# Centring image 0 ahead of the bias tables, a fourth warming product, and the step table made inside pairs 3 to 6

## The chip, the cores and the metric

One core of a Trainium2 chip runs the kernel. The metric is the device time of one execution in microseconds (us), as the median of several runs. The engines are TensorE (PE in the rows, with its weight loads as PEld), VectorE (DVE), ScalarE (ACT), GpSimd (POOL) and SyncE (SP), which here issues transfers. Each engine works through its own queue in order, and they wait for each other by semaphores.

## The reference

The input x is 4 images of 64 channels and 32 x 32 positions, in float32. Two blocks with residual additions follow each other.

```python
# 1: a layer norm over channels, then local attention over 7x7 windows
x = x + conv(ln_c(x), wq, wk, wv, rel_x, rel_y)
#    q, k, v = 1x1 projections; logits = q . k over the window + bias_x + bias_y
#    (from q and the two tables of relative positions); softmax over 49; mix v
# 2: 1024 tokens an image, a layer norm over channels, then 33 steps of a routed network
t = tokens(x)
t = t + ffn(ln_t(t), ...)
def step(h, p):
    op = argmax(h[0, 0, :19])            # one of 19 operations, from the state itself
    y = attention(h, wq[op], wk[op], wv[op]) @ wo[op];  h = where(attn_mask[op], y, h)
    z = relu(h @ w1[op] + b1[op]) @ w2[op] + b2[op];    h = where(ffn_mask[op], z, h)
```

At most steps both masks of the chosen operation are off and the state stays as it is. So the kernel makes a step table: for each operation and each step, the next step at which one of the two masks is on, and which of them.

## The kernel before

The work is a written-out queue for each engine. Channels lie on partitions, and two images lie above each other, so that [128, 1024] holds a pair of images; "image 0" below is the first such pair (x0_loaded) and "image 1" the second (x1_loaded). Both together are four quarters of 512 columns, numbered 0 to 3.

**The head** makes the normalised images for the first attention. For quarter j, centre(j) is one product of 128 x 128 by 512 columns on TensorE (x minus its mean over channels, L332), square(k, j) on ScalarE squares it (L750) and copies it out (L752), variance(k, j) on TensorE sums (L341), root(k, j) on ScalarE takes the root (L756), inverse(k, j) on VectorE the reciprocal (L1012), spread(k, j) on TensorE spreads it over the channels (L350), and scale(k, j) on VectorE multiplies (L1023). Then come the query products (L380), the bias products (biases, L401 and L404) and the scores.

TensorE's queue begins with three warming products of 512 columns on zeros (L362). Behind them it waits for the three small loads behind t_loaded (w_qk, w_q, bias_tables), turns the key weights (L366), makes the bias tables (L368), waits for ScalarE's copy of the turned keys (wk_copied, L769), folds the key weights into the query weights (L372) and signals tab_ready. Only then come centre(0), centre(1), variance(0, 0), the wait for image 1, centre(2), variance(0, 1), spread(0, 0), the wait for the copied tables (tab_copied), spread(0, 1), centre(3) and so on. ScalarE's queue has the key copy, the four table copies (L772, L774), and then square(0, 0), square(0, 1), root(0, 0), square(0, 2), root(0, 1), four copies of masks (L786), square(0, 3).

VectorE's queue has make_table() ahead of inverse(0, 0): thirteen small instructions (L993 to L1006) on 19 partitions, each but the last waited for by the next through dve_step. The last signals table_ready; SyncE writes the table out (L257) and reads it back as one row (L259). Its readers are all at the first decision, behind pair 15.

**The pairs.** The first attention is 16 pairs of blocks, p = 0 to 15. In round p TensorE turns the probabilities of pair p (L466), turns the values of pair p + 1 (L455), makes the scores of pair p + 2 (L441, L445) and mixes pair p (L478). VectorE's queue in round p is normalise(p + 1) (L1062, L1065), copy_values(p + 1) (L1074), maxima(p + 2) (L1056), add_mixed(p) (L1082). ScalarE takes the exponentials (L813) and copies (L824), and GpSimd copies the values of a pair (L313).

**Behind the pairs** come the second norm and the steps of the routed network.

Of the kernel before, what the change touches and what calls it, by code (L numbers as in the profile page):

```python
# [28 lines left out]
P = 128  # L29
C = 64  # L30
# [11 lines left out]
TX, TY = 32 + KC - 1, 32 + KR - 1  # L42
NBLK = NPOS // (BR * BC)
NB, NOPS, HID = 33, 19, 256
# [12 lines left out]
def build(nc, x, w_qk, w_q, w_v, bias_tables, key_onehot, masks, ident, mean_mat, spread_mat, iotas,  # L57
          attn_mask, ffn_mask, attn_pack, ffn_w1, ffn_pack, out):
    with ExitStack() as ctx:
# [3 lines left out]
        def sem(name):  # L63
            return ctx.enter_context(nc.semaphore(name))

        ps = ctx.enter_context(nc.psum_tensor("ps", [P, 8, 512], F32))


        eye = sb("eye", [P, P])
# [7 lines left out]
        wqk = sb("wqk", [C, P])  # L77
        wqk_bd = sb("wqk_bd", [P, P])
        wq_nat = sb("wq_nat", [C, C])
        wk_nat = sb("wk_nat", [C, C])  # L80
        wv_bd = sb("wv_bd", [P, P])
        rel_tab = sb("rel_tab", [C, TX + TY])
# [31 lines left out]
        ahead = sb("ahead", [NOPS, 2, 2 * NB])  # L114
        ahead_i = sb("ahead_i", [NOPS, NB + 1], I32)
# [34 lines left out]
        S = {n: sem(n) for n in names}  # L150
# [178 lines left out]
        def _(pe):  # L329
            def centre(j):  # L330

                nc.tensor.matmul(ps[:, j, :], centre_w[:], x2f[:, j * 512:j * 512 + 512],  # L332
                                 start=True, stop=True).then_inc(S["centred"], 1)

            def variance(k, j):

                pe.wait_ge(S["squared"], 4 * k + j + 1)
                if j >= 2:
                    pe.wait_ge(S["h_ready" if k else "normed"], j - 1)
                for s in range(4):  # L340
                    mm = nc.tensor.matmul(ps[32 * s:32 * s + 32, 4 + 2 * (j % 2), 0:P], mean_w[:, P:P + 32],  # L341
                                          sq[:, j * 512 + P * s:j * 512 + P * s + P], start=True, stop=True)
                mm.then_inc(S["var_ready"], 1)
# [14 lines left out]
                                     start=True, stop=True)  # L358

            pe.wait_ge(S["idle_set"], 1)  # L360
            for i in range(3):
                nc.tensor.matmul(ps[:, 6, :], idle_in[:, 0:P], idle_in[:], start=True, stop=True)  # L362

            pe.wait_ge(S["t_loaded"], 48)
            pe.wait_ge(S["eye_loaded"], 16)
            nc.tensor.transpose(ps[0:C, 5, 0:C], wqk[:, C:P], eye[0:C, 0:C]).then_inc(S["wk_turned"], 1)  # L366
            for h in range(2):
                nc.tensor.matmul(ps[C * h:C * h + C, 7, 0:TX + TY], wq_nat[:], rel_tab[:],  # L368
                                 start=True, stop=True)
            pe.wait_ge(S["wk_copied"], 1)  # L370
            for h in range(2):
                mm = nc.tensor.matmul(ps[C * h:C * h + C, 7, P:P + C], wq_nat[:], wk_nat[:],  # L372
                                      start=True, stop=True)
            mm.then_inc(S["tab_ready"], 1)

            def queries(j):

# [33 lines left out]
            pe.wait_ge(S["x0_loaded"], 32)  # L411
            centre(0)
            centre(1)
            variance(0, 0)
            pe.wait_ge(S["x1_loaded"], 32)
            centre(2)
            variance(0, 1)
# [325 lines left out]
        def _(act):  # L743
            def load_table(func):

                nc.scalar.activation(spare[:, 0:1], eps_c[:, 0:1], func)

            def square(k, j):
                act.wait_ge(S["centred"], 4 * k + j + 1)
                nc.scalar.activation(sq[:, j * 512:j * 512 + 512], ps[:, j, :],  # L750
                                     ACT.Square).then_inc(S["squared"], 1)
                nc.scalar.copy(xc[:, j * 512:j * 512 + 512], ps[:, j, :]).then_inc(S["centre_copied"], 1)  # L752

            def root(k, j):
                act.wait_ge(S["var_ready"], 4 * k + j + 1)
                nc.scalar.activation(sq[:, j * 512:j * 512 + P], ps[:, 4 + 2 * (j % 2), 0:P], ACT.Sqrt,  # L756
                                     bias=eps_c[:, k:k + 1]).then_inc(S["std_ready"], 1)
# [6 lines left out]
            act.dma_start(x2[C:P, 1], x_parts[1][1]).then_inc(S["x1_loaded"], 16)  # L764
            act.wait_ge(S["eps_set"], 1)
            load_table(ACT.Sqrt)
            act.wait_ge(S["w_zeroed"], 1)
            act.wait_ge(S["wk_turned"], 1)
            nc.scalar.copy(wk_nat[:], ps[0:C, 5, 0:C]).then_inc(S["wk_copied"], 1)  # L769
            act.wait_ge(S["tab_ready"], 1)  # L770
            for h in range(2):
                nc.scalar.copy(tabs[C * h:C * h + C, h, :], ps[C * h:C * h + C, 7, 0:TX + TY]  # L772
                               ).then_inc(S["tab_copied"], 1)
                nc.scalar.copy(wqk_bd[C * h:C * h + C, C * h:C * h + C], ps[C * h:C * h + C, 7, P:P + C]  # L774
                               ).then_inc(S["tab_copied"], 1)
            square(0, 0)
            square(0, 1)
            root(0, 0)
            square(0, 2)
            root(0, 1)  # L780
            act.wait_ge(S["c_loaded"], 64)
# [189 lines left out]
        def _(dve):  # L971
# [7 lines left out]
            dve.wait_ge(S["eye_loaded"], 16)  # L979
            nc.vector.tensor_tensor(centre_w[:], eye[:], mean_w[:, 0:P], ALU.subtract).then_inc(S["centre_ready"], 1)  # L980

            def make_table():


                steps = [0]

                def step(ins):
                    steps[0] += 1
                    ins.then_inc(S["dve_step"], 1)
                    dve.wait_ge(S["dve_step"], steps[0])  # L990

                dve.wait_ge(S["m_loaded"], 48)
                step(nc.vector.memset(ahead[:], 4.0 * NB))  # L993
                step(nc.vector.tensor_copy(kinds[:], masks8[:]))
                step(nc.vector.scalar_tensor_tensor(kinds[:, 0, :], kinds[:, 1, :], 2.0, kinds[:, 0, :],
                                                    ALU.mult, ALU.add))
                step(nc.vector.tensor_scalar(kinds[:, 1, :], kinds[:, 0, :], 0.0, 4.0 * NB,
                                             ALU.is_equal, ALU.mult))
                step(nc.vector.tensor_tensor(kinds[:, 0, :], kinds[:, 0, :], iota[:], ALU.add))
                step(nc.vector.tensor_tensor(ahead[:, 0, 0:NB], kinds[:, 0, :], kinds[:, 1, :], ALU.max))  # L1000
                by, at = 1, 0
                while by < NB:
                    step(nc.vector.tensor_tensor(ahead[:, 1 - at, 0:NB], ahead[:, at, 0:NB],
                                                 ahead[:, at, by:by + NB], ALU.min))
                    by, at = 2 * by, 1 - at
                nc.vector.tensor_copy(ahead_i[:], ahead[:, at, 0:NB + 1]).then_inc(S["table_ready"], 1)  # L1006

            def inverse(k, j):

                rstd = sq[:, j * 512:j * 512 + P]  # L1010
                dve.wait_ge(S["std_ready"], 4 * k + j + 1)
                nc.vector.reciprocal(rstd, rstd).then_inc(S["inv_ready"], 1)  # L1012

            def scale(k, j, done="normed"):
                at, bank = j * 512, 4 + 2 * (j % 2)
                dve.wait_ge(S["centre_copied"], 4 * k + j + 1)
                dve.wait_ge(S["spread_ready"], 4 * k + j + 1)
                if k == 0:
                    r0 = 16 * (j % 2)
                    dst = h_in[:, j // 2, r0:r0 + 16, :].rearrange("p (b r) w -> p b r w", b=2)  # L1020
                else:
                    dst = h2[:, at:at + 512].rearrange("p (b r w) -> p b r w", b=2, w=WW)
                nc.vector.tensor_tensor(dst,  # L1023
                                        xc[:, at:at + 512].rearrange("p (b r w) -> p b r w", b=2, w=WW),
                                        ps[:, bank:bank + 2, 0:256].rearrange("p b (r w) -> p b r w", w=WW),
                                        ALU.mult).then_inc(S[done], 1)

            make_table()
            dve.wait_ge(S["pads_set"], 1)
            inverse(0, 0)  # L1030
            inverse(0, 1)
            scale(0, 0)
            scale(0, 1)
            inverse(0, 2)
# [43 lines left out]
            def add_mixed(p):  # L1078
                b2, hb, xb = p // 8, p % 8 // 2, p % 2
                dve.wait_ge(S["pv_done"], p + 1)  # L1080
                win = x2[:, b2:b2 + 1, BR * hb:BR * hb + BR, BC * xb:BC * xb + BC]
                nc.vector.tensor_tensor(win, win,  # L1082
                                        ps[:, 7, 0:P].rearrange("p (a r c) -> p a r c", a=1, c=BC),
                                        ALU.add).then_inc(S["mixed"], 1)
# [9 lines left out]
            for p in range(1, NPAIR - 2):  # L1094
                normalise(p + 1)
                copy_values(p + 1)
                if p < 3:
                    add_bias(1, p - 1)
                maxima(p + 2)
                add_mixed(p)  # L1100
                if p == 7:
                    for h in range(2):
                        for at in range(2):
                            ins = nc.vector.tensor_copy(twice_w[C * h:C * h + C, C * at:C * at + C],
                                                        eye[C * h:C * h + C, C * h:C * h + C])
                    ins.then_inc(S["twice_set"], 1)
# [235 lines left out]
```

## Time and profile before

| | |
|---|---|
| median of 3 runs | 248.5 us (248.47 to 250.22) |
| the profiled execution's own time | 249.26 us |
| its span | 247.0 us |
| TensorE busy | 230.8 us, 93% of the span |
| VectorE busy | 161.4 us, 65% |
| ScalarE busy | 151.1 us, 61% |
| GpSimd busy | 25.5 us, 10% |
| mean granted TensorE clock | 0.991 of full speed |

The span is what the trace covers; the execution's own time is 2.26 us more. In the rows below times are microseconds from the start of the span. In a row of a timeline stand the start, the duration, the engine, the line of the kernel, the operation, what is written and read, and in brackets how long the engine sat idle before it and what ended that. The granted clock of TensorE has two levels, 1.2 and 2.4 GHz, which are 0.50 and 1.00 in the column PEclk.

### The profile page before, as it was taken

To read this page: it belongs to the slowest core of one execution; us is meant where nothing else is said; L and a number is where in the kernel's file an instruction comes from. 1 tells how busy PE (TensorE), PEld (TensorE's weight loads), DVE (VectorE), ACT (ScalarE), POOL (GpSimd) and SP (SyncE) were. 2 spreads that over 40 slices of the span, in tenths; PEclk is the share of its full clock that TensorE was granted. 3 is DMA by queue.
4 is the path that set the end of the run, shared out by engine and by line. 5 is a ranking of instruction groups with operands and counts; after the bars stand their busy time and mean duration, and the time that the engine had idled before them with its cause. 6 is when DMAs were issued, how large, how long until landed. Compare 5 with 4: busy or idle time off the path is not lost.

```text
span 247.0 us, 5393 instructions
## 1 busy us (share of the span) xinstructions
PE 230.8 (93%) x1999; PEld 155.2 (63%) x2000; DVE 161.4 (65%) x300; ACT 151.1 (61%) x291; POOL 25.5 (10%) x37
## 2 busy tenths in 40 slices
PE   7679989999999998999899999999999999998991
PEld 3236658766777755533375787788888888886330
DVE  1535645676776644764596999897778778762642
ACT  2174462446456685464459988879887876682641
POOL 9600032212122100160000000000000000000000
PEclk9889999999999999999999999999999999999998
DMA  6500000000000001000100000000000000000006
GB/s 157 126 1 3 3 0 3 5 0 0 3 0 3 0 0 36 1 0 13 33 0 0 3 0 4 1 3 0 3 0 3 0 3 0 3 0 4 0 22 149
DMA packets 3151, 3.60 MB, mean 15 GB/s; under 512 B 1077, under 2 KB 2229, under 8 KB 3126
## 3 DMA queue, kind: packets, MB, share of 16 engines
q1 hardware_dynamic: 2486, 2.59, 4.4%
q10 hardware_dynamic: 544, 0.66, 1.0%
q8 instruction: 16, 0.26, 0.4%
q14 instruction: 9, 0.07, 0.1%
q0 software_dynamic: 96, 0.00, 0.0%
HBM read 2.21 MB, written 1.05 MB: 13 GB/s over the span
## 4 chain that ended last, share of the span: by engine, by line
PE 77%; DVE 6%; ACT 6%; issue 4%; DMA 2%; ACTq 2%; DVEq 1%
PE ps L649 12%; PE ps L635 11%; PE ps L614 11%; PE ps L702 6%; PE ps L716 6%; PE ps L478 5%; PE ps L466 4%; PE ps L441 4%; PE ps L332 3%; PE ps L445 3%; DMA rel_tab<-in_bias_tables 2%; PE ps L401 2%; DVE sq L1012 2%; ACT prob L813 2%; PE ps L455 1%
## 5 line engine op out<-in xcount | busy, mean ns | idle before, releaser
L935 ACT COPY arena<-ps 128x1024 f32<-128x1024 f32 x32 | 32.3, 1010 | 15.8 <-PE ps L635 15.6
L1155 DVE TENSOR_REDUCE negmax<-ps 128x1 f32<-128x1024 f32 x32 | 38.4, 1218 | 1.3 <-PE ps L614 1.1
L614 PE MATMUL ps<-h_st,g_st 128*128 128x512 f32 x128 | 38.6, 423 | 0.7 <-ACT late L883 0.4
L883 ACT ACTIVATE late<-ps,negmax 128x1024 f32<-128x1024 f32 x32 | 35.8, 1119 | 5.1 <-DVE negmax L1155 4.5
L635 PE MATMUL ps<-eye,late 128*128 128x128 f32 x256 | 33.5, 274 | 0.6 <-DVE late L1165 0.2
L635 PEld LDWEIGHTS ps<-eye,late 128*128 128x128 f32 x256 | 29.1, 141 | 6.9 <-DVE late L1165 2.7
L813 ACT ACTIVATE prob<-ps,negmax 128x308 f32<-128x308 f32 x32 | 16.3, 513 | 27.7 <-DVE negmax L1056 27.7
L649 PE MATMUL ps<-arena,late 128*64 128x128 f32 x512 | 31.5, 276 | 1.1 <-ACT arena L935 1.1
L649 PEld LDWEIGHTS ps<-arena,late 128*64 128x64 f32 x512 | 27.6, 137 | 3.8 <-issue 2.2
L614 PEld LDWEIGHTS ps<-h_st,g_st 128*128 128x128 f32 x128 | 21.7, 188 | 8.8 <-issue 3.2
L1165 DVE TENSOR_SCALAR late<-late,rinv 128x1024 f32<-128x1024 f32 x32 | 24.1, 754 | 1.1
L313 POOL TENSOR_TENSOR v_st<-arena,ones_c 128x308 f32<-128x308 f32 x16 | 11.1, 701 | 61.1 <-PE ps L455 36.1
L950 ACT ACTIVATE arena<-ps,w2p 128x512 f32<-128x512 f32 x16 | 11.0, 687 | 9.0 <-PE ps L702 9.0
L478 PEld LDWEIGHTS ps<-prob_t,v_key 103*64 103x64 f32 x192 | 10.2, 136 | 9.1 <-ACT prob_t L824 4.1
L702 PE MATMUL ps<-h,w1d 64*128 64x512 f32 x64 | 15.7, 617 | 0.1
L478 PE MATMUL ps<-prob_t,v_key 103*64 103x128 f32 x192 | 14.0, 281 | 1.6 <-ACT arena L803 1.1
L1056 DVE TENSOR_REDUCE negmax<-ps 128x2 f32<-128x616 f32 x16 | 12.7, 793 | 3.8 <-PE ps L445 3.8
L716 PE MATMUL ps<-arena,w2p 128*64 128x512 f32 x64 | 15.1, 602 | 0.0
L824 ACT COPY prob_t<-ps 103x384 f32<-103x384 f32 x32 | 13.7, 487 | 2.1 <-PE ps L466 2.1
L466 PE MATMUL ps<-eye,prob 128*103 128x128 f32 x96 | 14.4, 286 | 0.0
L1162 DVE RECIPROCAL rinv<-rowsum 128x1 f32<-128x1 f32 x32 | 5.2, 161 | 13.1 <-ACT late L883 12.2
L1065 DVE TENSOR_SCALAR prob<-prob,rinv 128x308 f32<-128x308 f32 x32 | 13.1, 451 | 0.6
(120 smaller groups left out, 318.9 us busy)
## 6 DMA issues: line engine op xcount, KB each, us to landing
out<-osum SPq DMA_DIRECT2D x8, 128.0 KB, 2.3
x<-in_x SPq DMA_DIRECT2D x2, 256.0 KB, 5.0
x<-in_x ACTq DMA_DIRECT2D x2, 256.0 KB, 6.0
onehot<-in_key_onehot SPq DMA_DIRECT2D x2, 133.0 KB, 2.8
w1d<-in_ffn_w SPq DMA_DIRECT2D x4, 64.0 KB, 2.4
w2p<-in_ffn_pack SPq DMA_DIRECT2D x2, 65.5 KB, 2.6
spread_w<-in_spread_mat SPq DMA_DIRECT2D x4, 32.0 KB, 5.5
mean_w<-in_mean_mat SPq DMA_DIRECT2D x1, 96.0 KB, 2.3
```

What stands on the lines that cost most here:

```text
L466: mm = nc.tensor.transpose(ps[0:CH, 4 + h, c * P:c * P + P], prob[:, pp, h, c * CH:c * CH + CH], eye[:])
L478: mm = nc.tensor.matmul(ps[C * h:C * h + C, 7, 0:P], v_key[0:CH, pp, c, C * h:C * h + C], prob_t[0:CH, pp, h, c, :], start=(c == 0), stop= ...
L614: mm = nc.tensor.matmul(ps[:, 2 * h + c, :], g_st[:, b2, h, q0:q0 + P], h_st[:, b2, h, part, c * 512:c * 512 + 512], start=(part == 0), st ...
L635: mm = nc.tensor.transpose(ps[:, bank + i, (c % 4) * P:(c % 4) * P + P], pr[:, n % 2, c * P:c * P + P], eye[:])
L649: mm = nc.tensor.matmul(ps[C * h:C * h + C, 7, cols], vk[:, g // 2, c, C * h:C * h + C], prt[:, g % 2, h, c, cols], start=(c == 0), stop=( ...
L702: mm = nc.tensor.matmul(ps[:, set0 + 2 * h + c, :], w1d[C * h:C * h + C, c * P:c * P + P], h2[C * h:C * h + C, t * 512:t * 512 + 512], sta ...
L716: mm = nc.tensor.matmul(ps[C * h:C * h + C, set0 + first, :], w2p[:, c * C:c * C + C], hid[t % 2][:, 2 * h + c, :], start=(i == 0), stop=( ...
L813: ins = nc.scalar.activation(prob[:, pp, h, 0:NKEY], ps[:, 2 * pp + h, 0:NKEY], ACT.Exp, bias=negmax[:, pp, h:h + 1], accum_out=rowsum[:, ...
L883: nc.scalar.activation(pr[:, n % 2, :], ps[:, 2 * (n % 2):2 * (n % 2) + 2, :], ACT.Exp, bias=negmax[:, 0, n % 2:n % 2 + 1], accum_out=rows ...
L935: nc.scalar.copy(prt[:, n // 8 % 2, n % 2, :, q0:q0 + P], ps[:, bank:bank + 2, :].rearrange("p b (c q) -> p (b c) q", c=4)).then_inc(S["s_ ...
L1155: nc.vector.tensor_reduce(negmax[:, 0, n % 2:n % 2 + 1], ps[:, 2 * (n % 2):2 * (n % 2) + 2, :], mybir.AxisListType.XY, ALU.max, negate=Tru ...
L1165: nc.vector.tensor_scalar(pr[:, n % 2, :], pr[:, n % 2, :], rinv[:, 0, n % 2:n % 2 + 1], None, ALU.mult).then_inc(S["s_prob"], 1)
```

## The change

1. TensorE has four warming products where it had three.
2. TensorE issues centre(0) and centre(1) ahead of the bias tables. These are now two functions: tables() (the waits for the small loads, the turn and the table products) stands behind centre(1), and fold_keys() behind variance(0, 0).
3. ScalarE issues square(0, 0) ahead of the key copy, and square(0, 1) and root(0, 0) between the key copy and the four table copies.
4. make_table() is split into table_kinds(), table_ends() and table_fold(first, n), and they move from the head into VectorE's pair loop, each behind add_mixed(p): kinds in round 3, ends in round 4, three folds in round 5, three folds and the last cast in round 6. SyncE's two transfers of the table wait for table_ready as before.
5. The wait for pads_set on VectorE moves behind inverse(0, 1).

```diff
-            for i in range(3):
+            for i in range(4):
                 nc.tensor.matmul(ps[:, 6, :], idle_in[:, 0:P], idle_in[:], start=True, stop=True)
-            pe.wait_ge(S["t_loaded"], 48)
-            pe.wait_ge(S["eye_loaded"], 16)
-            nc.tensor.transpose(ps[0:C, 5, 0:C], wqk[:, C:P], eye[0:C, 0:C]).then_inc(S["wk_turned"], 1)
-            for h in range(2):
-                nc.tensor.matmul(ps[C * h:C * h + C, 7, 0:TX + TY], wq_nat[:], rel_tab[:],
-                                 start=True, stop=True)
-            pe.wait_ge(S["wk_copied"], 1)
...
+            def tables():
+                pe.wait_ge(S["t_loaded"], 48)
+                pe.wait_ge(S["eye_loaded"], 16)
+                nc.tensor.transpose(ps[0:C, 5, 0:C], wqk[:, C:P], eye[0:C, 0:C]).then_inc(S["wk_turned"], 1)
...
+            def fold_keys():
+                pe.wait_ge(S["wk_copied"], 1)
...
             centre(0)
             centre(1)
+            tables()
             variance(0, 0)
+            fold_keys()
             pe.wait_ge(S["x1_loaded"], 32)
             centre(2)
...
             load_table(ACT.Sqrt)
+            square(0, 0)
             act.wait_ge(S["w_zeroed"], 1)
             act.wait_ge(S["wk_turned"], 1)
             nc.scalar.copy(wk_nat[:], ps[0:C, 5, 0:C]).then_inc(S["wk_copied"], 1)
+            square(0, 1)
+            root(0, 0)
             act.wait_ge(S["tab_ready"], 1)
...
-            square(0, 0)
-            square(0, 1)
-            root(0, 0)
             square(0, 2)
...
+            def table_kinds():
                 dve.wait_ge(S["m_loaded"], 48)
                 step(nc.vector.memset(ahead[:], 4.0 * NB))
                 step(nc.vector.tensor_copy(kinds[:], masks8[:]))
...
+            def table_fold(first, n):
+                for i in range(first, first + n):
+                    by, at = 1 << i, i % 2
                     step(nc.vector.tensor_tensor(ahead[:, 1 - at, 0:NB], ahead[:, at, 0:NB],
                                                  ahead[:, at, by:by + NB], ALU.min))
+                    if 2 * by >= NB:
+                        nc.vector.tensor_copy(ahead_i[:], ahead[:, 1 - at, 0:NB + 1]
+                                              ).then_inc(S["table_ready"], 1)
...
-            make_table()
-            dve.wait_ge(S["pads_set"], 1)
             inverse(0, 0)
             inverse(0, 1)
+            dve.wait_ge(S["pads_set"], 1)
             scale(0, 0)
...
                 add_mixed(p)
+                if p == 3:
+                    table_kinds()
+                if p == 4:
+                    table_ends()
+                if p in (5, 6):
+                    table_fold(3 * (p - 5), 3)
```

## Rows read from the trace of the kernel before

**Rows 1.** The page: chain of waits, shares of the span by engine.

```profile
PE 77%; DVE 6%; ACT 6%; issue 4%; DMA 2%; ACTq 2%; DVEq 1%
```

**Rows 2.** The chain of waits in order of time: start, duration, what.

```profile
3.35 5.97 DMA rel_tab<-in_bias_tables
...
10.28 3.60 PE ps L332 x4
14.24 1.07 PE ps L332 x2
15.34 0.60 ACT sq L750
...
17.81 0.71 PE ps L350 x8
...
90.67 1.98 PE ps L332 x4
```

**Rows 3.** Timeline of TensorE in the head, the warming products.

```profile
1.44 5.49 PE L362 MATMUL ps<-idle_in 128*128 128x512 f32 x6 [1.44 <-DVE idle_in L972]
```

**Rows 4.** Windows: stretch, length, busy PE, PEld, DVE, ACT, POOL, PEclk, DMA, GB/s.

```profile
10.00:10.50 0.50, 0.50 (x5) 0.43 (x6) 0.43 (x3) 0.17 (x2) 0.00 (x0) 0.74 0.69 140
...
13.50:14.00 0.50, 0.50 (x9) 0.16 (x8) 0.00 (x0) 0.07 (x1) 0.00 (x0) 0.85 0.00 0
...
16.00:18.00 2.00, 0.91 (x11) 0.77 (x13) 1.61 (x3) 1.72 (x6) 0.00 (x0) 1.00 0.00 0
```

**Rows 5.** Timeline of ScalarE in the head.

```profile
9.70 0.20 ACT L769 COPY wk_nat<-ps 64x64 f32<-64x64 f32 x1 [3.56 <-PE ps L366]
10.33 0.23 ACT L772 COPY tabs<-ps 64x98 f32<-64x98 f32 x1 [0.43 <-PE ps L372]
...
10.84 0.21 ACT L774 COPY wqk_bd<-ps 64x64 f32<-64x64 f32 x1
...
14.88 0.38 ACT L756 ACTIVATE sq<-ps,eps_c 128x128 f32<-128x128 f32 x1
15.34 0.60 ACT L750 ACTIVATE sq<-ps 128x512 f32<-128x512 f32 x1
...
16.30 0.38 ACT L756 ACTIVATE sq<-ps,eps_c 128x128 f32<-128x128 f32 x1
```

**Rows 6.** Later halves of images 0 and 1: issue, and time to landing.

```profile
L760 ACTq DMA_DIRECT2D x<-in_x x1: 571/571/571, 1.2 to 1.2; - x1
...
DMA to landing us min/median/max: 5.9/5.9/5.9
...
L764 ACTq DMA_DIRECT2D x<-in_x x1: 617/617/617, 4.0 to 4.0; - x1
...
DMA to landing us min/median/max: 6.0/6.0/6.0
```

**Rows 7.** Timeline of VectorE: the two casts of the step table.

```profile
8.72 1.24 DVE L994 CAST kinds<-masks 19x66 f32<-19x66 uint8 x1
...
12.15 0.17 DVE L1006 CAST ahead_i<-ahead 19x34 int32<-19x34 f32 x1
```

**Rows 8.** Timeline of all engines in the pairs.

```profile
54.99 0.80 DVE L1056 TENSOR_REDUCE negmax<-ps 128x2 f32<-128x616 f32 x1 [0.42 <-PE ps L445]
...
65.20 0.17 DVE L1062 RECIPROCAL rinv<-rowsum 128x2 f32<-128x2 f32 x1 [0.88 <-ACT prob L813]
65.29 0.70 POOL L313 TENSOR_TENSOR v_st<-arena,ones_c 128x308 f32<-128x308 f32 x1 [3.42 <-PE ps L455]
65.40 1.06 DVE L1065 TENSOR_SCALAR prob<-prob,rinv 128x308 f32<-128x308 f32 x2
...
67.13 0.90 PE L466 MATMUL ps<-eye,prob 128*103 128x128 f32 x6
```

**Rows 9.** One line on VectorE: duration in ns, minimum, median, maximum.

```profile
L1065 DVE TENSOR_SCALAR prob<-prob,rinv x32: 368/380/771, 30.4 to 88.7; 128x308 f32<-128x308 f32 x32
```

More of the change, by code:

```diff
@@ L360, in _ @@
             pe.wait_ge(S["idle_set"], 1)
-            for i in range(3):
+            for i in range(4):
                 nc.tensor.matmul(ps[:, 6, :], idle_in[:, 0:P], idle_in[:], start=True, stop=True)
-            pe.wait_ge(S["t_loaded"], 48)
-            pe.wait_ge(S["eye_loaded"], 16)
-            nc.tensor.transpose(ps[0:C, 5, 0:C], wqk[:, C:P], eye[0:C, 0:C]).then_inc(S["wk_turned"], 1)
-            for h in range(2):
-                nc.tensor.matmul(ps[C * h:C * h + C, 7, 0:TX + TY], wq_nat[:], rel_tab[:],
-                                 start=True, stop=True)
-            pe.wait_ge(S["wk_copied"], 1)
[L371 to L374, printed above, removed]
+            def tables():
+                pe.wait_ge(S["t_loaded"], 48)
+                pe.wait_ge(S["eye_loaded"], 16)
+                nc.tensor.transpose(ps[0:C, 5, 0:C], wqk[:, C:P], eye[0:C, 0:C]).then_inc(S["wk_turned"], 1)
+                for h in range(2):
+                    nc.tensor.matmul(ps[C * h:C * h + C, 7, 0:TX + TY], wq_nat[:], rel_tab[:],
+                                     start=True, stop=True)
+            def fold_keys():
+                pe.wait_ge(S["wk_copied"], 1)
+                for h in range(2):
+                    mm = nc.tensor.matmul(ps[C * h:C * h + C, 7, P:P + C], wq_nat[:], wk_nat[:],
+                                          start=True, stop=True)
+                mm.then_inc(S["tab_ready"], 1)
             def queries(j):
@@ L980, in _, with step @@
             nc.vector.tensor_tensor(centre_w[:], eye[:], mean_w[:, 0:P], ALU.subtract).then_inc(S["centre_ready"], 1)
[L982 to L990, printed above, removed]
+            steps = [0]
+            def step(ins):
+                steps[0] += 1
+                ins.then_inc(S["dve_step"], 1)
+                dve.wait_ge(S["dve_step"], steps[0])
+            def table_kinds():
                 dve.wait_ge(S["m_loaded"], 48)
@@ L996, in make_table, with table_ends @@
                                                     ALU.mult, ALU.add))
+            def table_ends():
                 step(nc.vector.tensor_scalar(kinds[:, 1, :], kinds[:, 0, :], 0.0, 4.0 * NB,
@@ L1000, in make_table @@
                 step(nc.vector.tensor_tensor(ahead[:, 0, 0:NB], kinds[:, 0, :], kinds[:, 1, :], ALU.max))
-                by, at = 1, 0
-                while by < NB:
+            def table_fold(first, n):
+                for i in range(first, first + n):
+                    by, at = 1 << i, i % 2
                     step(nc.vector.tensor_tensor(ahead[:, 1 - at, 0:NB], ahead[:, at, 0:NB],
                                                  ahead[:, at, by:by + NB], ALU.min))
-                    by, at = 2 * by, 1 - at
-                nc.vector.tensor_copy(ahead_i[:], ahead[:, at, 0:NB + 1]).then_inc(S["table_ready"], 1)
+                    if 2 * by >= NB:
+                        nc.vector.tensor_copy(ahead_i[:], ahead[:, 1 - at, 0:NB + 1]
+                                              ).then_inc(S["table_ready"], 1)
             def inverse(k, j):
```

## The prediction

> **What bounds the kernel now.** I read the chain of waits first: TensorE is on it for 77% of the span [rows 1], so anything that lets TensorE's long stretches start sooner shortens the whole, unless a later wait eats it. Then the same chain in order of time for the head [rows 2]. The reader should see five links: the load of the bias tables, issued at 3.35 and landed 5.97 us later, at 9.32; a stretch to 10.28 in which TensorE makes the tables; the two centring products of image 0, 3.60 us; then centre 2 at 14.24, ScalarE's square at 15.34; and the spread of quarter 1 at 17.81, from which TensorE runs on without a gap into the bias products. Image 0 itself has long been there: the last half of it is issued at 1.2 and lands 5.9 us later, at 7.1 [rows 6]. So centring waits some 3 us behind a load that it doesn't need.
>
> Third, the clock. Two centring products take 3.60 us at 10.28 and 1.98 us at 90.67 [rows 2]. The granted clock falls inside 10.00 to 10.50 (mean 0.74, so at about 10.24) and is back inside 13.50 to 14.00 (mean 0.85, about 13.65) [rows 4]: the centring products ran at 1.2 GHz, with TensorE idle before them. The three warming products take 5.49 us from 1.44 to 6.93, 1.83 each [rows 3]: the low pace too, though the record shows no low clock there. A clock that falls at 10.24 must have been high before, so it rose near the end of the warming or just behind it.
>
> **Centring first, behind a fourth warming product.** Removed: TensorE's idle time to 9.32 and the low clock under the centring. The fourth product begins behind 6.93. At the high pace a product is 0.99 us (1.98 / 2) [rows 2], at the low one 1.83 [rows 3]: it ends between 7.9 and 8.8. I take 7.9, since the clock must have risen by about 7; 8.8 stays in the range. Image 0 is there at 7.1, so the product costs TensorE's start 0.8 us. By 1.98 for two products, centre 0 is done at 8.9 and centre 1 at 9.9.
>
> ScalarE's queue then sets the pace. Steps from [rows 5]: a square with its copy 0.96 (15.34 to 16.30), a root 0.46 (14.88 to 15.34), the copy of the turned keys 0.20, the four copies of the tables 0.72 (10.33 to 10.84 + 0.21). In the new order:
> - square 0 from 8.9 to 9.85;
> - the key copy: TensorE turns the keys behind centre 1, and before, this copy began 0.38 after the landing at 9.32. Behind 9.9 it would start at 10.3 at the latest, and at 9.85 if square 0 alone held it. I take 10.0, done at 10.2;
> - square 1 from 10.2 to 11.1; root 0 to 11.6; table copies to 12.3; square 2 to 13.2; root 1 at 13.2. Steps on this queue overlap by some 0.05 each, which brings it to about 13.0.
>
> It was 16.30 [rows 5]. TensorE is never later than this: tables and folding took 0.96 before (9.32 to 10.28), variance 0 0.36 (13.88 to 14.24), centre 2 1.07 [rows 2]; from 9.9 these add up to 12.3, and ScalarE wants centre 2 at 12.3. Centre 2 needs image 1, issued at 4.0 and landed 6.0 later, at 10.0 [rows 6]: in time. From root 1 to the spread of quarter 1 went 1.5 us (16.30 to 17.81), with VectorE's inverse between; that stays. So the gain at the spread is 3.1 to 3.3 us: 3.8 or so at root 0 (14.88 to 11.1), of which the four table copies, now between root 0 and square 2, take 0.7, and the squares' waits for the low-paced products, now gone, give some back. I take 3.2. The tables are ready at 12.3, and their first user is the spread's wait at about 14.5: no cost.
>
> **The step table out of the head.** In the head it ended at 12.32 (12.15 + 0.17) [rows 7], while VectorE's first inverse had waited for a root since. It was free there. With root 0 now at about 11.5 it would have held the first inverse by 0.8 us, yet the spread hangs on the second, behind root 1, so even that would hardly have been felt. Taking it out is worth 0 to 0.2 us.
>
> **The step table in pairs 3 to 6.** Thirteen instructions. From the cast's start to the last one's end 3.6 us for twelve of them (8.72 to 12.32) [rows 7], 0.2 for the memset; but the cast's 1.24 us fell beside GpSimd's memsets, and the other cast took 0.17. Otherwise they step by some 0.21. The parts are 3, 3, 3 and 4 instructions: 0.6, 0.6, 0.6 and 0.85 us. Each is queued behind the addition of a pair's result, where VectorE now idles 0.88 us for an exponential (the same in each of the four pairs), and further on, behind pairs 3 to 5, it idles 0.42 before the maxima [rows 8]. Queued behind a part are the normalisation and, through it, TensorE's turning of the probabilities. The tightest case is behind pair 6: its idle time is 0.88 before 65.20, the normalisation ends at 66.46 (65.40 + 1.06), and the turn starts at 67.13, 0.67 later [rows 8]. A part decides only from 0.88 + 0.67 = 1.55 us. Price taken: 0; bound from above, if the first part holds a cast of 1.24, 1.65 us of VectorE in a pair with 0.88 + 0.42 idle and a later-due reader: 0.1. Below nothing: none, since no engine waits for VectorE there. SyncE's two transfers of the table move from 12.35 to about 62; SyncE has nothing behind them but its wait for the first decision, at 90.
>
> **A page against a row.** VectorE's normalising product takes 380 ns in the median and up to 771 [rows 9], the long ones where GpSimd copies values (65.29, for 0.70, beside the 1.06 us of 65.40) [rows 8]. The Trainium skill, SBUF — State Buffer, section "SBUF: two separate sides", says why that may be: one pair of ports is an exclusive lock between VectorE and GpSimd, and whichever comes second blocks for the whole instruction. That speaks against putting casts inside the pairs. The rows answer it: the gap of 0.88 ends at 65.20, before GpSimd begins at 65.29; and one collision costs at most 0.70, a part of 1.3 to 1.55, still not above 1.55.
>
> **The sum.** The profiled execution took 249.26, its span 247.0. 249.26 - 3.2 - 0.1 + 0.1 = 246.06; I forecast 246.0. The profiled run lies inside the spread of the three shown (248.47 to 250.22, median 248.5), a spread of 1.75, near the 1.6 by which centring at the low clock differs from the high (3.60 - 1.98). So I read the profiled execution as a middling one and make no correction for the profile; if it carries one, the result is 248.5 - 3.2 = 245.3. Against the median the forecast is 1.0% faster, about the size that a measurement of this kernel can tell from no change.
>
> **Rivals.**
> - *The clock doesn't stay up.* TensorE has idle time behind the variance of quarter 1: busy 0.91 of 2.00 us in 16.00 to 18.00, at clock 1.00 [rows 4], and with the table copies ahead of square 2 the gap gets about 0.8 longer. Or the rise comes late, and part of the centring runs at 1.2 GHz again. Either costs 1.0 to 1.7 us: 247.0 to 247.7. For it: it fell once in this head. Against it: it held through an only half-busy stretch. The Trainium skill, TensorE: Matmul & The Clock Gate, section "Part 1: The HAM clock gate", says that the same kernel shows different counts of cold matmuls from run to run; that makes this rival come and go between executions, and would narrow the spread of the changed kernel where the fourth product covers it.
> - *The gain is eaten by the next late thing.* Key copy or image 1 late by transfers that were hidden (landing at 10.0, wanted at 10.6): 1 us less gain, 247.0.
> - *It doesn't do what it says:* later waits fall on fixed times, nothing moves: 248.5. I see none; every stretch behind the head hangs on the one before.
> - *Slower: the parts land on the path.* Place: pairs 3 to 6, behind the addition. If the exponentials are late by a part's whole length, all 3.8 us come back: 249.26 - 3.2 + 3.8 = 249.9; from 1.55 us a part it decides. With collisions of 0.70 in three of them, 252.
>
> **Chances.** Forecast (245.0 to 246.8) 0.62; clock 0.15; eaten 0.12; no effect 0.06; slower mechanism 0.05, of which 0.03 over 251. Range 245.0 to 247.7: from the case of a profile's surplus to the clock rival. Faster by over 1% (below 246.0) takes half of everything, since the forecast sits on that bound: 0.50; within 1% 0.47; slower 0.03.
>
> **What the profile would show.** Four warming products ending at 7.9; centring from there in 2.0 us with no fall of the clock by 14; root 1 near 13.0, the spread of quarter 1 near 14.5; in pairs 3 to 6 the idle 0.88 shrunk to 0.3 or 0, and the pairs' period unchanged. Wrong if the centring takes 3.6 again, if the table load lands over 1 us later, or if TensorE waits for VectorE in pairs 3 to 6.

## The result, and the profile after

The changed kernel took 245.61 us in the median of 4 executions (245.45 to 246.76), the kernel before 248.67 beside it (248.47 to 250.22): a ratio of 0.986, 95% interval 0.983 to 0.989. The forecast was 246.0 in a range of 245.0 to 247.7. The profiled execution took 245.56 with a span of 243.4, where that of before took 249.26 with a span of 247.0.

First the chain of waits of the changed kernel in order of time, for [rows 2]:

```profile
1.44 6.10 PE ps L362 x8
7.54 0.87 PE ps L332 x2
...
8.44 0.60 ACT sq L757
...
9.53 0.21 ACT wk_nat L777
...
10.70 0.26 ACT sq L763
...
12.66 0.28 ACT sq L763
...
12.96 0.96 DVE sq L1025
...
14.06 0.72 PE ps L350 x8
...
86.94 1.98 PE ps L332 x4
```

The load of the bias tables is gone from it, and the four warming products stand in it instead (1.44 to 7.54). Image 0 was there before they ended; the source view of its last half:

```profile
L767 ACTq DMA_DIRECT2D x<-in_x x1: 571/571/571, 1.2 to 1.2; - x1
...
DMA to landing us min/median/max: 5.1/5.1/5.1
```

It landed at 6.3 (1.2 + 5.1). The reader should see ScalarE from 8.44 to 12.94 instead, with hardly a break: squares (L757), the key copy (L777), roots (L763) and, between 10.96 and 11.56, the table copies. The spread of quarter 1 stands at 14.06, 3.75 us earlier than in [rows 2]; at the centring behind the first decision the lead is 3.73 (90.67 to 86.94), and in the span 3.6. What the head gained went through the whole kernel, but for 0.15.

The timeline of TensorE, for [rows 3] and for the gap between the two first spreads:

```profile
1.44 6.10 PE L362 MATMUL ps<-idle_in 128*128 128x512 f32 x8 [1.44 <-DVE idle_in L979]
...
7.38 1.88 PE L332 MATMUL ps<-x,centre_w 128*128 128x512 f32 x4
...
12.09 0.71 PE L350 MATMUL ps<-sq,spread_w 64*128 64x128 f32 x8 [0.32 <-DVE sq L1025]
...
14.06 0.72 PE L350 MATMUL ps<-sq,spread_w 64*128 64x128 f32 x8 [1.25 <-DVE sq L1025]
```

And the windows, for [rows 4]:

```profile
10.00:10.50 0.50, 0.50 (x9) 0.40 (x6) 0.00 (x0) 0.50 (x2) 0.00 (x0) 1.00 0.78 140
...
13.50:14.00 0.50, 0.00 (x0) 0.00 (x0) 0.50 (x2) 0.47 (x2) 0.00 (x0) 1.00 0.00 0
```

Two centring products take 1.88 us, not 3.6, and the clock stays at 2.4 GHz. Four warming products take 6.10 us where three took 5.49, 1.83 each: the pace rose under them.

The timeline of VectorE in pairs 3 and 6, for [rows 7] and [rows 8]:

```profile
48.19 0.17 DVE L999 MEMSET ahead<- 19x132 f32 x1
48.39 0.18 DVE L1000 CAST kinds<-masks 19x66 f32<-19x66 uint8 x1
...
49.17 0.17 DVE L1074 RECIPROCAL rinv<-rowsum 128x2 f32<-128x2 f32 x1 [0.38 <-ACT prob L820]
...
61.13 0.17 DVE L1018 CAST ahead_i<-ahead 19x34 int32<-19x34 f32 x1
...
61.45 0.17 DVE L1074 RECIPROCAL rinv<-rowsum 128x2 f32<-128x2 f32 x1
```

The first cast, 1.24 us in the head, takes 0.18 here; behind the part of pair 3 VectorE still idles 0.38 us; the part of pair 6 fills the gap to the end. From the addition of pair 3 to that of pair 15 it is 42.22 us in both kernels (51.68 to 93.90 before, 47.94 to 90.16 after): the parts cost nothing.

### The profile page after: what moved, and what is told of

It reads as the page before. It is cut to its first block, busy times and chain, and to the rows that moved or that the text cites. A ratio compares the mean times of both kernels' runs of the same rounds, so it can differ in the third digit from the quotient of the medians.

```text
span 243.4 us, 5399 instructions
## 1 busy us (share of the span) xinstructions
PE 229.4 (94%) x2001; PEld 155.4 (64%) x2002; DVE 159.9 (66%) x300; ACT 151.0 (62%) x291; POOL 25.5 (10%) x37
## 4 chain that ended last, share of the span: by engine, by line
PE 79%; ACT 8%; DVE 7%; issue 4%; DVEq 1%; ACTq 1%
PE ps L656 12%; PE ps L642 11%; PE ps L621 11%; PE ps L709 6%; PE ps L723 6%; PE ps L485 5%; PE ps L473 4%; PE ps L448 4%; PE ps L452 3%; PE ps L362 3%; PE ps L406 2%; DVE sq L1025 2%; ACT prob L820 2%; PE ps L332 2%; PE ps L462 1%
## 5 line engine op out<-in xcount | busy, mean ns | idle before, releaser
L1025 DVE RECIPROCAL sq<-sq 128x128 f32<-128x128 f32 x8 | 7.3, 937 | 13.3 <-ACT sq L763 11.4
L1180 DVE RECIPROCAL rinv<-rowsum 128x1 f32<-128x1 f32 x32 | 5.2, 161 | 13.2 <-ACT late L890 12.2
```

## The experiments

All twelve were timed beside the kernel before. The clock of an execution is its mean granted TensorE clock; it sorts the executions of the kernel before and of the changed kernel, so it stands with them. It is a rough measure, though. It also counts low stretches behind the last product, where they cost nothing (in the trace of the changed kernel from about 241.8 to the end), and it stands at 1.00 under the first warming products, where the pace is low (1.83 us a product, for 0.99 at the high clock). In e5, 245.80 us goes with 1.0 and 246.97 with 0.997, and the two longest executions of e8 have 1.0.

```
kernel                                  us, each execution (clock)
before, beside e1 to e4, 20 executions  248.07-248.95 (0.989-0.993) x9, 249.5-250.07 (0.985-0.986) x10, 251.73 (0.976)
before, beside e5 to e8, 23 executions  246.87 (0.997), 248.12-249.44 (0.990-0.993) x16, 249.83-250.29 (0.985-0.986) x5, 251.57 (0.976)
before, beside e9 to e12, 11 executions 248.21-249.00 (0.990-0.992) x7, 249.52-249.99 (0.985-0.986) x4
changed, first timing                   245.45 245.56 245.66 (0.997), 246.76 (0.991)
changed, again (e9)                     245.31 245.34 245.46 245.51 245.79 (0.994-0.998), 246.91 (0.990)
```

### One warming product less (e1)

```diff
-            for i in range(4):
+            for i in range(3):
                 nc.tensor.matmul(ps[:, 6, :], idle_in[:, 0:P], idle_in[:], start=True, stop=True)
```

> The changed kernel with three warming products instead of four; nothing else differs. In the changed kernel the fourth ends at 7.54 and image 0 lands at about 7.1, and ScalarE meets its next stop, the copy of the turned keys, at 9.53 because the table load lands at 9.19. Theory (order, with the clock covered by the centring itself): centring starts 0.3 us earlier, ScalarE waits longer for the keys, so within 0.3 us of the changed kernel: 245.4 to 245.9. Rival (the fourth product is what holds the clock up): the clock rises late or falls, the centring takes up to 3.6 us instead of 1.9, so 246.5 to 247.5, with a low clock in the trace between 7 and 14.

Measured: median 246.72, ratio 0.987 (0.983 to 0.992), in two groups: 245.02 and 245.34 at a clock of 0.996 and 0.994, and 246.45 to 247.22 (four) at 0.989 to 0.991. Its profiled execution, 247.0, is of the second. Timeline of TensorE:

```profile
1.44 4.29 PE L362 MATMUL ps<-idle_in 128*128 128x512 f32 x6 [1.44 <-DVE idle_in L979]
7.29 1.95 PE L332 MATMUL ps<-x,centre_w 128*128 128x512 f32 x4 [1.56 <-DMA x<-in_x]
...
14.05 0.71 PE L350 MATMUL ps<-sq,spread_w 64*128 64x128 f32 x8 [1.25 <-DVE sq L1025]
14.70 2.07 PE L332 MATMUL ps<-x,centre_w 128*128 128x512 f32 x2
```

and its windows:

```profile
14.50:15.00 0.50, 0.50 (x7) 0.38 (x4) 0.13 (x1) 0.00 (x0) 0.00 (x0) 0.65 0.00 0
15.00:18.00 3.00, 3.00 (x11) 0.90 (x11) 0.56 (x1) 1.17 (x3) 0.00 (x0) 0.50 0.00 0
```

Both expectations missed. The centring ran at the high clock, in 1.95 us, though TensorE had idled 1.56 before it; so in this execution the fourth product is not what keeps it fast. But the clock fell inside 14.50 to 15.00, behind the gap of 1.25 us, and centre 3 took 2.07 instead of 1.12. The rival had the right size and the wrong place. The two executions without the fall, at 245.02 and 245.34, are 0.2 to 0.5 below the 245.5 of the changed kernel, as the theory had it. Two times in the expectation are misread: in the changed kernel image 0 landed at 6.3, not 7.1, and the table load at 8.8 (3.3 + 5.5); 9.19 is where TensorE, done with the centring, turns the keys.

### The step table back in the head (e2)

```diff
+            table_kinds()
+            table_ends()
+            table_fold(0, 6)
             inverse(0, 0)
             inverse(0, 1)
...
-                if p == 3:
-                    table_kinds()
-                if p == 4:
-                    table_ends()
-                if p in (5, 6):
-                    table_fold(3 * (p - 5), 3)
```

> The changed kernel with the whole step table back ahead of the first inverse. It would end at about 12.2, while root 0 is there at 10.96: the first inverse is 1.2 us late and ends at 13.2, the second starts there instead of 12.96. Theory (the spread of quarter 1 hangs on root 1 alone): 0.2 to 0.3 us slower than the changed kernel, 245.8 to 246.0. Rival (the head is VectorE-bound once the centring is early, so moving the table was what paid): 1.2 us slower, 246.8.

Measured: median 245.58 (245.56 to 245.83), ratio 0.985 (0.981 to 0.989), all at a clock of 0.995 to 0.998. Timeline of TensorE:

```profile
7.13 1.88 PE L332 MATMUL ps<-x,centre_w 128*128 128x512 f32 x4
...
13.34 1.53 PE L350 MATMUL ps<-sq,spread_w 64*128 64x128 f32 x16 [1.81 <-DVE sq L1025]
14.79 1.12 PE L332 MATMUL ps<-x,centre_w 128*128 128x512 f32 x2
```

and from its chain of waits:

```profile
7.79 2.20 DVE kinds L1000
...
12.34 0.87 DVE sq L1025
```

The first inverse is late, and both spreads run together at 13.34. From centre 0 to centre 3 it is 7.66 us (7.13 to 14.79), in the changed kernel's trace 7.33 (7.38 to 14.71). So the table in the head costs 0.3 in the trace, as the theory had it, and nothing that the medians tell. The move is not what paid. But in e2 the chain of waits runs through the step table, whose cast takes 2.20 us beside GpSimd's memsets: the table is done at 12.34, and the second inverse starts behind the first. So with a shorter queue on ScalarE, as in e8, the table in the head should cost more; that was not run.

### Only the clock of the kernel before (e3 and e4)

```diff
-            for i in range(3):
+            for i in range(4):      # e4: range(6)
                 nc.tensor.matmul(ps[:, 6, :], idle_in[:, 0:P], idle_in[:], start=True, stop=True)
```

> The kernel before with a fourth warming product and nothing else. The warming ends near 7.6 to 8.7 instead of 6.93, the table load lands at 9.3 as before. Theory (the order is needed as well): TensorE still idles 0.7 to 1.8 us, then makes the tables first; if the clock stays up, 1.5 us faster than before (247.1), if it falls, no change (248.6). I expect a mixture, 247.8. Rival (the fourth product alone brings the gain): 245.6.

> The kernel before with six warming products: TensorE is busy until about 9.2, where the table load lands, so that the centring runs at the high clock while its order stays that of before. Theory: the clock is worth 1.7 us at the centring, of which 1.5 reach the end: 247.1, and the other 1.5 us of the gain belong to the order. Rival (the clock is all): 245.6. Rival (the order is all, ScalarE hides the low clock): 248.6.

Measured: e3 247.12 (246.83 to 247.83, nine), ratio 0.991 (0.988 to 0.995), all at 0.995 to 0.999. e4 247.30, ratio 0.994 (0.991 to 0.998): eight at 246.85 to 247.59 (0.997 to 0.999) and four at 249.2 to 249.7 (0.990 to 0.991). Timeline of TensorE in e3:

```profile
8.63 0.24 PE L366 MATMUL ps<-eye,wqk 64*64 64x64 f32 x1 [1.91 <-DMA rel_tab<-in_bias_tables]
...
9.49 1.98 PE L332 MATMUL ps<-x,centre_w 128*128 128x512 f32 x4
...
15.40 0.71 PE L350 MATMUL ps<-sq,spread_w 64*128 64x128 f32 x8 [0.51 <-DVE sq L1012]
```

and in e4:

```profile
8.68 0.24 PE L366 MATMUL ps<-eye,wqk 64*64 64x64 f32 x1 [0.15 <-DMA rel_tab<-in_bias_tables]
...
9.54 1.98 PE L332 MATMUL ps<-x,centre_w 128*128 128x512 f32 x4
```

In the order of before, with the high clock under the centring, the kernel takes 247.0 to 247.2, as expected of e4. That is 1.5 above the changed kernel (the worth of the order) and 1.5 to 2.4 below the medians of before, 248.67 to 249.53 (the worth of the clock). The one execution of before that had a clock of 0.997 agrees: 246.87. The traces add a reservation: in e3 and e4 the table load landed 5.2 and 5.3 us after its issue, for 5.97 in the trace of before, so centring began some 0.7 earlier. Of the 2.41 us by which the second spread of e3 is earlier (17.81 to 15.40) this is 0.7, and the clock 1.7. Whether the landing is scatter can't be told from two traces; in e7 it took 5.8, in the changed kernel 5.5. Neither part alone is the gain. e3 came out at the good end of its mixture: the idle time, 1.91 us in the trace, did not bring the mean clock under 0.995 in any of nine. Why four of e4's twelve are longer no trace shows.

### The step table in one piece (e5 and e6)

```diff
-                if p == 3:
-                    table_kinds()
-                if p == 4:
-                    table_ends()
-                if p in (5, 6):
-                    table_fold(3 * (p - 5), 3)
+                if p == 3:          # e6: p == 6
+                    table_kinds()
+                    table_ends()
+                    table_fold(0, 6)
```

> The changed kernel with all thirteen instructions of the step table in one piece behind the addition of pair 3: 2.75 us on VectorE. By the arithmetic of the prediction: the gap before the normalisation is 0.88 and TensorE turns those probabilities 1.6 us after the normalisation's end, so 2.5 us are covered there; the piece is 0.25 longer. Theory: 0.1 to 0.4 us slower than the changed kernel, 245.7 to 246.0. Rival (the idle time is not needed in one stretch, later slack absorbs all): no difference, 245.6. Rival (only the gap of 0.88 covers it): 1.9 us slower, 247.5.

> The same piece of 2.75 us behind the addition of pair 6, where the cover is 0.88 + 0.67 = 1.55 us. Theory: TensorE's turn of the next probabilities waits for VectorE by about 1.2 us, of which nothing comes back: 246.8, with an idle time of TensorE behind pair 7 that ends on VectorE. Rival (absorbed by later pairs, as they run close to ScalarE's and VectorE's own pace): 245.6.

Measured: e5 245.97 (245.80 to 246.97), ratio 0.989 (0.986 to 0.993); e6 247.73 (247.16 to 249.48), ratio 0.996 (0.993 to 0.999). In the traces the stretch from the addition of pair 3 to that of pair 15 grew from 42.22 to 42.97 in e5 (48.44 to 91.41), by 0.75; from that of pair 6 it grew from 29.88 to 31.73 in e6 (60.52 to 92.25), by 1.85. Timeline of all engines in e6:

```profile
61.78 0.70 POOL L313 TENSOR_TENSOR v_st<-arena,ones_c 128x308 f32<-128x308 f32 x1 [3.42 <-PE ps L462]
61.84 0.69 DVE L1009 TENSOR_TENSOR ahead<-kinds 19x33 f32<-19x33 f32 x1
...
64.87 0.90 PE L473 MATMUL ps<-eye,prob 128*103 128x128 f32 x6 [1.17 <-DVE prob L1077]
...
67.92 0.77 PE L485 MATMUL ps<-prob_t,v_key 103*64 103x128 f32 x10 [0.57 <-ACT prob_t L831]
```

and of TensorE in e5:

```profile
52.78 0.90 PE L473 MATMUL ps<-eye,prob 128*103 128x128 f32 x6 [0.27 <-DVE prob L1077]
```

The piece took 3.25 us in both (60.78 to 64.03 in e6), not 2.75: one of its instructions took 0.69 instead of 0.18 beside GpSimd's copy. Less the margins, 1.55 in the prediction and 2.5 in the expectation of e5, that leaves 3.25 - 1.55 = 1.70 for e6 and 3.25 - 2.5 = 0.75 for e5, and the traces have 1.85 and 0.75. The median of e6 came out 0.9 above what was expected, that of e5 inside its 245.7 to 246.0. e5's is only 0.4 to 0.5 above the medians of the changed kernel, less than the 0.75; its profiled execution, 246.78, also has a head 0.5 later (48.44 for 47.94), since its warming products took 6.60 us. That the sums agree so well is in part luck, for the price is made up otherwise than by them. TensorE's first wait, 1.17 us in e6, is on the normalisation, which runs in 0.67 instead of 1.06 now that it no longer meets GpSimd's copy. The rest comes a round later: VectorE has no idle time left there, its maxima and with them ScalarE's exponentials are late, and TensorE waits 0.57 for a copied block of probabilities. In e5, too, only 0.35 of the 0.75 stands at the turn of the probabilities, and the rest in the products behind it. By the traces the rivals that had all absorbed, or only the gap of 0.88 as cover in pair 3, fall.

### The step table alone (e7)

```diff
-            make_table()
             dve.wait_ge(S["pads_set"], 1)
             inverse(0, 0)
...
                 add_mixed(p)
+                if p == 3:
+                    table_kinds()
...
```

> The kernel before with the step table alone moved into pairs 3 to 6. In its head the table ended 3.05 us before the first inverse had its root. Theory: no change in the head and none in the pairs, 248.6 (248.4 to 249.2). Rival (the parts cost in the pairs): up to 1 us slower, 249.6. Rival (the table held the head): faster.

Measured: 249.78 (246.84 to 250.43, twelve), ratio 1.003 (0.9995 to 1.006): no difference that this can tell. Its executions fall in the groups of before: one at 246.84 (0.997), four at 248.95 to 249.41 (0.990 to 0.992), seven at 249.78 to 250.43 (0.985 to 0.986). From the addition of pair 3 to that of pair 15 its trace has 42.22 us (51.41 to 93.63), like both kernels. TensorE's timeline shows the centring half in the low clock:

```profile
10.04 2.93 PE L332 MATMUL ps<-x,centre_w 128*128 128x512 f32 x4
```

It takes 3.60 in the trace of before and 2.93 here, in the same queue with the same waits: where the clock turns differs from execution to execution. The median above that of before, 248.79, comes from more executions at 0.985, seven of twelve here for five of 23; beside e1 to e4 before had ten of 20.

### Root 1 ahead of the table copies (e8)

```diff
             fold_keys()
+            variance(0, 1)
             pe.wait_ge(S["x1_loaded"], 32)
             centre(2)
-            variance(0, 1)
...
             square(0, 1)
             root(0, 0)
+            root(0, 1)
             act.wait_ge(S["tab_ready"], 1)
...
             square(0, 2)
-            root(0, 1)
```

> A further step on the changed kernel: TensorE sums variance 1 ahead of centre 2, and ScalarE takes root 1 directly behind root 0, ahead of the four table copies and of square 2. If the new head is bound by ScalarE's queue from 8.44 to 12.9, as the chain of waits of the changed kernel says, root 1 starts 1.6 us earlier, VectorE's second inverse follows the first directly (at 11.95 instead of 12.96) and the spread of quarter 1 starts 1.0 us earlier: 244.6. Rival (something else stands right behind, such as the landing of image 1 or the table copies that the spread waits for): under 0.4 us, 245.3.

Measured: 244.34 (243.94 to 244.94), ratio 0.983 (0.979 to 0.986). Chain of waits in order of time:

```profile
3.34 5.77 DMA rel_tab<-in_bias_tables
...
9.16 0.26 PE ps L368
...
10.96 0.96 DVE sq L1025
...
12.06 0.71 PE ps L350 x8
...
12.87 0.71 PE ps L350 x8
13.59 1.05 PE ps L332 x2
```

The second spread starts at 12.87 instead of 14.06. The new bound was ScalarE's queue, as the chain of the changed kernel said, and this version beats both kernels. Its chain also shows what comes next: the load of the bias tables is back at its start, landed at 9.11, because the key copy stands ahead of square 1 in ScalarE's queue.

### The gap and the clock (e9 to e12)

e9 is the changed kernel once more. e10 adds a filler to it, e11 the same filler with three warming products, e12 is e8 with three warming products.

```diff
             spread(0, 0)
+            keep_busy(3, 2)         # e10, e11: two products of 256 columns on zeros
             pe.wait_ge(S["tab_copied"], 4)
             spread(0, 1)
```

> The changed kernel itself once more, for the spread of its executions beside those of the next three. So far three lay at 245.45 to 245.66 with a mean clock of 0.997 and one at 246.76 with 0.991. Theory (in some executions the clock falls behind the 1.25 us gap of TensorE between the two first spreads, whatever the number of warming products): a median of 245.6, and one in three or four executions at 246.5 to 247.2 with a mean clock near 0.990. Rival (the fourth product is what separates it from the version with three): all six within 245.4 to 245.9.

> The changed kernel with two products of 256 columns on zeros (as the kernel uses elsewhere to keep TensorE busy) put between the spread of quarter 0 and that of quarter 1, where TensorE idles 1.25 us. Theory (the gap lets the clock fall in some executions): the median stays at 245.6, no execution above 246.0, mean clock 0.995 or more in each. Rival (the scatter comes from elsewhere): one in three still above 246.4. The fillers take 1.06 us, so at most 0.1 us is lost if the inverse is early.

> Three warming products and the same two fillers in the gap. In the version with three and no filler four of six executions lay at 246.45 to 247.22 and two at 245.02 and 245.34, and its trace had the low clock from 14.65 to 18.06. Theory: all six go to 245.0 to 245.6, so the fourth product isn't needed for the clock once the gap is filled. Rival (a missing fourth product lets the clock rise late, in the centring): executions above 246 remain.

> The version with root 1 ahead of the table copies, and three warming products. There the second spread follows the first without a gap, so by the theory of the gap no filler is needed: 244.0 to 244.6 in all executions, within 0.3 us of the version with four. Rival (three warming products are too few by themselves): a group of executions 1.2 to 2 us higher.

Measured: e9 245.49 (245.31 to 246.91), ratio 0.986 (0.983 to 0.988). e10 245.83 (245.57 to 245.93), ratio 0.987 (0.984 to 0.989), clock 0.995 to 0.997. e11 245.53 (245.38 to 245.93), ratio 0.986 (0.983 to 0.989), clock 0.996 to 1.0. e12 244.29 (243.99 to 244.60), ratio 0.980 (0.978 to 0.983), clock 0.994 to 1.0. The profiled execution of e9 is the one at 246.91. Timeline of TensorE:

```profile
13.87 0.72 PE L350 MATMUL ps<-sq,spread_w 64*128 64x128 f32 x8 [1.26 <-DVE sq L1025]
14.51 1.88 PE L332 MATMUL ps<-x,centre_w 128*128 128x512 f32 x2
```

and windows:

```profile
11.00:13.00 2.00, 1.28 (x17) 0.71 (x16) 0.97 (x2) 1.94 (x7) 0.00 (x0) 1.00 0.11 37
13.00:15.00 2.00, 1.13 (x9) 0.86 (x10) 1.58 (x3) 0.80 (x3) 0.00 (x0) 0.94 0.00 0
15.00:17.00 2.00, 2.00 (x11) 0.30 (x9) 0.38 (x1) 0.57 (x2) 0.00 (x0) 0.50 0.00 0
```

This is the changed kernel itself with the clock falling behind its gap, as in e1: the longest execution is explained by its own trace. With the gap filled or closed (e8, e10, e11, e12) none of 21 executions has a mean clock under 0.994 and none forms a second group; with the gap open it is two of ten with four warming products and four of six with three. Four long executions of six in e1 against none of five in e11 would come by chance in one case of twenty, against the ten of e11 and e12 together in one of a hundred; for four products, five executions without such a one (e10) would come by chance in one case of three, so there it rests on the trace. The length of the gap is not the whole of the cause, though. e2 has one idle time of 1.81 us in place of 0.32 and 1.25, and e5 has the gap open as it is, and none of the six executions of either is under 0.995. e6 has it open too, and four of twelve at 0.993 and 0.994, whose cause no trace shows.

The median of e10 is 0.3 above that of e9. The filler is not seen to cost this. Chain of waits of e10, and its timeline of TensorE:

```profile
1.19 6.14 DMA x<-in_x
...
7.46 1.96 PE ps L332 x4
```

```profile
12.33 0.72 PE L350 MATMUL ps<-sq,spread_w 64*128 64x128 f32 x8 [0.31 <-DVE sq L1026]
...
14.30 0.71 PE L350 MATMUL ps<-sq,spread_w 64*128 64x128 f32 x8 [0.20 <-DVE sq L1026]
```

From spread to spread it is 1.97 us, as in the changed kernel (12.09 to 14.06); this execution is late because image 0 landed at 7.33. Where the 0.3 of the median comes from stays open.

## Why the prediction was right

**The bound.** The low clock and the needless wait for the tables in the head were as read: e3 and e4 take the low clock away and keep the wait, and land 1.5 us above the changed kernel.

**The sum at the spread.** Foreseen 3.2 us, 3.75 in the traces. The terms that were off: the fourth product ended at about 7.5, not 7.9, because the clock rose under it (square 0 at 8.44 for 8.9), and the key copy began at 9.53, for 10.0. The steps written down for ScalarE add up to 13.3 before the overlap is taken off, not 13.2. ScalarE's queue was as summed: from key copy to root 1 3.0 us were foreseen (10.0 to 13.0) and 3.02 measured (9.53 to 12.55). All of it reached the end but 0.15.

**The fourth product.** Foreseen to cost 0.8 us of TensorE's start, behind an image landing at 7.1, and to be there for the clock. In the changed kernel's trace image 0 had landed at 6.3 and the warming products ended at 7.54, so TensorE's start waited for them and they are on the chain. In the medians the fourth product costs 0.3 with the gap filled (245.83 in e10, 245.53 in e11) and nothing with root 1 first (244.34 in e8, 244.29 in e12). For the centring it wasn't needed in any of the three traces with three: 1.95, 2.02 and 1.96 us in e1, e11 and e12. Whether it makes the fall behind the gap rarer, two of ten against four of six, so few executions can't settle.

**The step table.** Out of the head 0 to 0.2, measured 0.3 in the trace and nothing in the median (e2); in the pairs 0, measured 0.00 (42.22 us in before, the changed kernel and e7). The margin of 1.55 us behind pair 6, and the 2.5 behind pair 3 that the expectation of e5 worked out the same way, fit the traces in their sums: pieces of 3.25 us cost 1.85 and 0.75. The rule that the prediction takes from the Trainium skill, SBUF — State Buffer, section "SBUF: two separate sides", that VectorE and GpSimd lock each other out, is borne out by the 0.69 us in e6; in the changed kernel no part meets GpSimd (the part of pair 6 ends at 61.30, GpSimd's copy begins at 61.54).

**The clock rival** is real and was priced about right: 1.2 to 1.4 us above the main group in two of ten executions, for 1.0 to 1.7. Its place was named too, the longer gap behind the variance of quarter 1. It doesn't move the median. The Trainium skill, TensorE: Matmul & The Clock Gate, section "Part 1: The HAM clock gate", has the same kernel cold for a different time from run to run. The traces agree, with four warming products taking 5.21 us in e9 and 6.60 in e5, and the centring in the order of before 3.60, or 2.93 in e7.

**Time against the median.** The profiled execution of before was taken as a middling one, and the sum was built on it. 54 further executions of before have groups at 0.990 to 0.993 and at 0.985 to 0.986, medians of 249.53, 248.79 and 248.96, and single ones at 246.87, 251.57 and 251.73; so 249.26 lay 0.3 above the middle. That it lay so near was luck as far as three executions could tell: the same gain taken from an execution at 246.87 or 251.73 would have given 243.7 or 248.5, both outside the range. The 246.0 was 0.4 above the 245.61 by the 0.45 of the first two terms.

## What to carry to other kernels

Read in a head what each queue waits for first, and ask of every load whether what stands behind it needs it; here the load of the tables stood ahead of the centring, and putting the centring first was worth 1.5 us by the medians, and the high clock about 1.7 by the traces of e3 and before. Behind such a move the next bound stands in the new chain of waits: here one engine's queue, and one exchange in it gave another 1.2 us. Small work fitted into an engine's regular idle time at no cost where it came in pieces no longer than that time (0.6 to 0.8 us into 0.88); one piece of 3.25 us cost 0.75 behind one pair and 1.85 behind another.

## What the runs showed of the hardware

A kernel of fixed work on one core scattered from 246.87 to 251.73 us, and the mean granted clock sorts its executions: 0.997, 0.990 to 0.993, 0.985, 0.976. A fall of the clock behind the gap of the head cost 1.2 to 1.4 us in the changed kernel. Whether an idle time of TensorE brings the clock down can't be read from its length alone. Idle times of 1.56 us (e1), 1.81 (e2) and 1.91 (e3) in one piece didn't, nor two of 0.32 and 1.25 in the profiled execution of the changed kernel; two of 0.32 and 1.26 in e9, in the same code with as much busy time around them (2.41 us of 11.00 to 15.00, for 2.43), did.
